# A three-stage attention kernel: six waits of the routed branch taken apart, and a causal mask moved from TensorE to VectorE

## The chip, the core and the metric

The kernel runs on one core of a Trainium2 chip. The metric is the device time of one execution in microseconds (us). A core has a matrix engine (TensorE, PE in the profile; PEld is its weight load), a vector engine (VectorE, DVE), an activation engine (ScalarE, ACT), a general engine (GpSimd, POOL) and a queue engine that starts transfers (SyncE, SP). Each runs its own list of instructions in order and waits for the others at semaphores. Matrix products land in PSUM, which has eight banks of 512 float32 numbers in each of 128 partitions.

## The reference

The input is one sequence of 2048 rows of 128 numbers. Three pieces matter here; the rest is an attention with relu weights (16 heads of 8) and a gated layer between the pieces.

```python
# routed branch: 255 of 2048 rows are chosen by a router weight, and get a layer of their own
weights = (x @ router_w)[..., 0] + router_b[0]
topv, topi = jax.lax.top_k(weights, k)
sel_idx = jnp.sort(topi[:, :kc], axis=1)
m_sel = m[bidx[:, :, None], sel_idx[:, :, None], sel_idx[:, None, :]]
sc = jnp.einsum('bhqd,bhkd->bhqk', q, kk) / np.sqrt(hd).astype(np.float32)
sc = sc + m_sel[:, None]
a = jax.nn.softmax(sc, axis=-1)
x2 = x1 + jax.nn.gelu(rmsnorm(x1, ln2) @ w1) @ w2

# second attention: 16 heads of 64, causal
q = jnp.einsum('bsm,hmd->bshd', x, W_Q) + b_Q
scores = jnp.einsum('bqhd,bkhd->bhqk', q, k) / jnp.sqrt(jnp.float32(D_HEAD))
causal = jnp.tril(jnp.ones((seq, seq), dtype=bool))
```

The masked scores go through a softmax, are multiplied with the values, and W_O maps them back to 128 numbers.

## The kernel before

The program is five blocks, one after the other; a block starts when every engine has ended the one before. `prepare` (0 to about 44.8 us) normalises, projects, and counts for each row how many router weights are larger. It also stores q and k, each as a high and a low part, to DRAM, and SyncE waits for these four stores before the block ends. `routed0` (to about 120.8 us) is the routed branch. Then come the relu attention (`attention0`), `between`, and from about 550 us `attention1`, the second attention.

**prepare.** `HIGHS_AFTER` and `LOWS_AFTER` say after which of the 16 comparisons of the counting ScalarE copies the high parts and VectorE subtracts the low parts; units 4 to 7 are those of k. Each store starts when its four parts are there.

**routed0.** VectorE makes 16 one-hot tiles (L877), and TensorE gathers the chosen rows with them (L1052). Meanwhile GpSimd sums twelve of the tiles (`tails`, L865 to 868). TensorE selects columns of the mask (L1063), ScalarE copies them out (L1010, two copies of two banks each, then kT, L1013), and TensorE selects rows (L1129) into one bank for both halves s of the queries. VectorE copies the result (L941) and adds it to the scores (L955); ScalarE takes the exponentials (L1026). Behind the last head VectorE writes the reciprocal of the sums, spread over the 8 columns of each head (L965), TensorE transposes it (L1172), ScalarE copies it out (`share`, L1033), VectorE scales (L969) and TensorE mixes (L1179). Between L1172 and the mixing TensorE also does `place(0)` to `place(3)`: transposes of the one-hot tiles (L1077) for the scatter at the end. Then come a norm with a square root on ScalarE (L1038), a product (L1193), a gelu over 1024 columns (L1040) and a product (L1199).

**attention1.** The 8 pairs of heads go through 10 groups of 4 steps each; a step is one tile of 128 keys against up to 512 queries, of both heads. TensorE's work with PSUM is a list of units (`UNIT`) that share three pairs of banks in turn: unit n may start when unit n-3 is freed. The units are scores (freed by ScalarE's exponential, L1895), projections, values, mixes, turns, and maximum tiles. A maximum tile is a tile of 128 queries against up to 512 keys (L1731); VectorE takes its row maxima (L1952) and frees the unit. These are for the pair of heads that comes next. A pair has 40 of them; 16 lie on the diagonal, four each with 128, 256, 384 and 512 columns. In a diagonal tile TensorE adds the mask to the last 128 columns with four bfloat16 products of 128 columns (L1736). VectorE also takes the reciprocal of the sums (L1973) and multiplies with it (L1976), in the same list.

A maximum tile is written (i, c) below: i the tile of queries (0 to 15), c the block of 512 keys; it is diagonal where c is i // 4.

Of the kernel before, what the change touches and what calls it, by code (L numbers as in the profile page):

```python
# [78 lines left out]
def prepare(nc, a, sh):  # L79

    with ExitStack() as ctx:
# [63 lines left out]
        HIGHS_AFTER = {2: range(NC, 2 * NC)}  # L145
        LOWS_AFTER = {1: range(0, 2), 2: range(2, NC), 10: range(NC, 2 * NC)}
# [285 lines left out]
def attention0(nc, a, sh):  # L432

    with ExitStack() as ctx:
# [78 lines left out]
        def _(pool):  # L513
# [19 lines left out]
            second_constants(nc, link, sh, sh.xnT)  # L533
# [174 lines left out]
def routed0(nc, a, sh):  # L708


    with ExitStack() as ctx:
# [106 lines left out]
        PLACE_BANK = [0, 1, 2, 3, 2, 3, 5, 6]  # L818
# [27 lines left out]
        def _(pool):  # L846
# [17 lines left out]
            pool.wait_ge(ranked, T - MT)  # L864
# [6 lines left out]
        def _(dve):  # L871
# [68 lines left out]
            dve.wait_ge(mask_taken, 1)  # L940
            link(nc.vector.tensor_copy(mask_sel[:, :, 0:SEL],  # L941
                                       bank[7].rearrange("p (s k) -> p s k", s=NS)[:, :, 0:SEL]))
# [7 lines left out]

            for n in range(H):
                if n % GH == 0:
                    dve.wait_ge(scored, n // GH + 1)
                for s in range(NS):
                    last = nc.vector.tensor_tensor_reduce(  # L955
                        out=prob[:, head(n), s, :], in0=bank[n % GH][:, s * SLOTS:(s + 1) * SLOTS],
                        in1=mask_sel[:, s, :], scale=-1.0, scalar=3.0e38, op0=ALU.add, op1=ALU.min,
                        accum_out=top[:, head(n), s:s + 1])
                last.then_inc(masked, 1)
# [15 lines left out]
            take_turned(1, bank[7])  # L975
# [5 lines left out]
            link(nc.vector.tensor_tensor(proc[:, :, :], bank[4][:, 0:NS * D].rearrange("p (s d) -> p s d", s=NS),  # L981
# [15 lines left out]
        def _(act):  # L997
# [10 lines left out]
            for n in range(2):  # L1008
                act.wait_ge(cols_taken, n + 1)
                nc.scalar.copy(mask_cols[:, 2 * n:2 * n + 2, :], sh.psum[:, 2 * n:2 * n + 2, 0:SLOTS])\  # L1010
                    .then_inc(cols_out, 1)
# [35 lines left out]
        def _(pe):  # L1047
# [92 lines left out]
            def turn_probs(n):  # L1140
# [3 lines left out]
                if n == 2:  # L1144
                    pe.wait_ge(qm_done, RES)
# [1017 lines left out]
```

## Time and profile before

| | us |
|---|---|
| median of 3 timed runs | 1413.13 (1411.38 to 1413.79) |
| the profiled execution, its own time | 1410.19 |
| its span in the trace | 1408.2 |
| PE busy | 1313.0 (93%) |
| DVE busy | 1015.9 (72%) |
| granted TensorE clock, mean | 0.982 |

The profile is of one execution. The 2 us between its own time and its span lie around the program. Busy shares are averages over stages with different limits, so the rows further down are read stage by stage: a row of the timeline gives the start, the duration, the engine, the line, what is written from what, and in brackets how long the engine had been idle before it and what ended that. The chain of waits is followed back from the last instruction, at each step to what released it.

### The profile page before, as it was taken

How to read it: one execution, taken by the hardware profiler on the slowest of the kernel's cores; microseconds unless marked ns; L12 is line 12 of the kernel's file. 1: busy time of each engine (PE TensorE's matmuls, PEld its weight loads, DVE VectorE, ACT ScalarE, POOL GpSimd, SP SyncE). 2: the span in 40 equal slices, each digit the busy share in tenths (PEclk: the TensorE clock that was granted, in tenths of full speed). 3: DMA queues.
4: the chain of work that ended last, by engine and by line, in shares of the span. 5: the costliest groups of instructions: out<-in, count | busy, mean ns of one | idle time of the engine just before them, and what ended most of it. 6: DMA issues, size and time to landing. Idle time of an engine off the chain costs nothing.

```text
span 1408.2 us, 25489 instructions
## 1 busy us (share of the span) xinstructions
PE 1313.0 (93%) x9902; PEld 674.9 (48%) x9902; DVE 1015.9 (72%) x1495; ACT 749.8 (53%) x1200; POOL 691.9 (49%) x527
## 2 busy tenths in 40 slices
PE   5778999999999987989999999999999999999897
PEld 3654222222222245555555655555555555555554
DVE  7666888888888875776766766766766666766768
ACT  5275777877777774334444444444344344344343
POOL 4301060100100010558678678677677677777671
PEclk9799999999999999999999999999999999999999
DMA  2511320000000000000000000000000000000000
GB/s 98 160 74 51 111 47 1 1 1 1 2 1 2 2 1 1 1 1 1 1 1 1 1 1 1 1 1 0 1 1 1 1 1 1 1 1 1 1 16 16
DMA packets 18166, 21.50 MB, mean 15 GB/s; under 512 B 7785, under 2 KB 15873, under 8 KB 16513
## 3 DMA queue, kind: packets, MB, share of 16 engines
q1 hardware_dynamic: 18048, 19.88, 4.6%
q8 instruction: 81, 1.33, 0.4%
q14 instruction: 37, 0.30, 0.1%
HBM read 14.63 MB, written 5.24 MB: 14 GB/s over the span
## 4 chain that ended last, share of the span: by engine, by line
PE 43%; DVE 11%; ACT 3%; issue 1%; POOL 1%; DVEq 0%; POOLq 0%; ACTq 0%
PE psum L1810 13%; PE psum L1788 12%; DVE part_max L1952 4%; PE psum L1731 4%; DVE inv L1973 4%; PE psum L1791 3%; ACT prob L1895 3%; PE psum L1769 2%; PE psum L1718 2%; PE psum L1757 2%; PE psum L1709 1%; DVE z L1976 1%; PE psum L1711 1%; PE psum L1710 1%; PE psum L1736 1%
## 5 line engine op out<-in xcount | busy, mean ns | idle before, releaser
L1698 POOL TENSOR_TENSOR acc<-acc,prob 128x1024 f32<-128x1024 f32 (+3 forms) x250 | 492.8, 1971 | 87.4 <-ACT prob L1895 57.6
L1895 ACT ACTIVATE prob<-psum 128x1024 f32<-128x1024 f32 (+1 forms) x320 | 283.3, 897 | 353.8 <-PE psum L1791 346.4
L1952 DVE TENSOR_REDUCE part_max<-psum 128x2 f32<-128x1024 f32 (+2 forms) x320 | 336.7, 1063 | 170.0 <-PE psum L1731 85.6
L696 DVE TENSOR_SCALAR w<-psum 128x512 f32<-128x512 f32 x472 | 304.7, 686 | 59.0 <-PE psum L553 46.6
L647 ACT ACTIVATE w<-psum 128x512 f32<-128x512 f32 x552 | 294.2, 600 | 85.4 <-PE psum L553 84.8
L573 PE MATMUL psum<-w,v_cols 128*32 128x512 f32 x2048 | 274.1, 608 | 0.0
L1810 PE MATMUL psum<-prob,v_pair 128*64 128x512 f32 (+3 forms) x1280 | 250.2, 532 | 0.7 <-POOL prob L1666 0.7
L1788 PE MATMUL psum<-q_hi,k_hi 64*128 64x512 f32 (+3 forms) x640 | 139.0, 430 | 30.4 <-DVE part_max L1952 21.5
L1810 PEld LDWEIGHTS psum<-prob,v_pair 128*64 128x64 f32 x1280 | 87.4, 137 | 145.2 <-issue 134.2
L1731 PE MATMUL psum<-k_hi,q_hi 64*128 64x512 f32 (+3 forms) x640 | 132.5, 411 | 6.0 <-DVE part_max L1952 4.4
L1788 PE MATMUL psum<-q_lo,k_hi 64*128 64x512 f32 (+3 forms) x640 | 119.1, 368 | 0.0
L1788 PE MATMUL psum<-q_hi,k_lo 64*128 64x512 f32 (+3 forms) x640 | 119.1, 368 | 0.0
L1791 PE MATMUL psum<-max_rows,ones_r 64*128 64x512 f32 (+3 forms) x640 | 118.7, 366 | 0.0
L1973 DVE RECIPROCAL inv<-psum 128x512 f32<-128x512 f32 x31 | 103.9, 3352 | 16.5 <-PE psum L1757 16.5
L553 PEld LDWEIGHTS psum<-q_rows,k_rows 32*128 32x128 f32 x768 | 40.3, 181 | 154.0 <-ACT w L647 148.1
L397 POOL TENSOR_SCALAR xa<-xa,rstd_j,shift_j 128x128 f32<-128x128 f32 x16 | 6.9, 449 | 209.0 <-DVE shift_j L389 209.0
L1666 POOL TENSOR_SCALAR_AFFINE_SELECT prob<-prob 128x256 f32<-128x256 f32 x128 | 53.3, 423 | 110.9 <-ACT prob L1895 110.1
L553 PE MATMUL psum<-q_rows,k_rows 32*128 32x512 f32 x768 | 101.6, 493 | 0.1
L1788 PEld LDWEIGHTS psum<-q_hi,k_hi 64*128 64x128 f32 x640 | 61.4, 188 | 78.0 <-DVE part_max L1952 47.4
L1731 PEld LDWEIGHTS psum<-k_hi,q_hi 64*128 64x128 f32 x640 | 61.2, 187 | 77.6 <-issue 40.8
L1694 POOL TENSOR_TENSOR acc<-prob 128x1024 f32<-128x1024 f32 x23 | 54.9, 2385 | 43.2 <-ACT prob L1895 41.4
L573 PEld LDWEIGHTS psum<-w,v_cols 128*32 128x32 f32 x2048 | 40.6, 108 | 63.8 <-ACT w L647 53.5
(301 smaller groups left out, 1411.3 us busy)
## 6 DMA issues: line engine op xcount, KB each, us to landing
q_rows<-q_dram SPq DMA_DIRECT2D x12, 256.0 KB
k_rows<-k_dram SPq DMA_DIRECT2D x3, 1024.0 KB
q_dram<-parts SPq DMA_DIRECT2D x2, 1024.0 KB, 4.2
k_dram<-parts SPq DMA_DIRECT2D x2, 1024.0 KB, 6.6
x<-in_L_attn_x SPq DMA_DIRECT2D x4, 256.0 KB, 4.0
mask<-in_L_ffn_attention_mask SPq DMA_DIRECT2D x1, 1024.0 KB, 6.0
x_high<-q_dram SPq DMA_DIRECT2D x4, 256.0 KB
x_low<-k_dram SPq DMA_DIRECT2D x1, 1024.0 KB
```

The costliest lines, as they stand in the source:

```text
L553: last = nc.tensor.matmul(pair_bank[n % RING][i], k_rows[group][rows, kt * P:(kt + 1) * P], q_rows[group][rows, qc * C:(qc + 1) * C], star ...
L573: last = nc.tensor.matmul(out_bank[turn % 2][h * VW:(h + 1) * VW, :], v_cols[group][:, kt, h, :], w[:, s % WR, h, :], start=(kt == 0), sto ...
L647: nc.scalar.activation(w[:, s % WR, 2 * m + i, :], pair_bank[n % RING][i], ACT.Relu)\
L696: nc.vector.tensor_scalar(w[:, s % WR, 2 * m + 1, :], pair_bank[n % RING][1], 0.0, None, ALU.max)\
L1698: nc.gpsimd.tensor_tensor(sums, sums, prob[:, s % PR, :, q0:C], ALU.add).then_inc(summed, 1)
L1731: last = nc.tensor.matmul(to[:, m, 0:n], q_hi[HALF[m], i * P:(i + 1) * P], k_hi[hp % 2][HALF[m], c * C:c * C + n], start=True, stop=not di ...
L1788: nc.tensor.matmul(to[:, m, q0:C], left[HALF[m], keys], right[HALF[m], at], start=n == 0, stop=False)
L1791: last = nc.tensor.matmul(to[:, m, q0:C], ones_r[HALF[m], :], max_rows[HALF[m], at], start=False, stop=True)
L1810: last = nc.tensor.matmul(out_bank[HALF[m], q0:C], v_pair[hp % 2][:, kt, HALF[m]], prob[:, s % PR, m, q0:C], start=kt == 0, stop=kt == (qc ...
L1895: nc.scalar.activation(prob[:, s % PR, :, q0:C], unit_both[n % RING][:, :, q0:C], ACT.Exp, scale=SCALE)\
L1952: nc.vector.tensor_reduce(part_max[:, :, i, c], unit_both[n % RING][:, :, 0:cols], AX_X, ALU.max)\
L1973: nc.vector.reciprocal(inv[:, :], side_bank).then_inc(inv_done, 1)
```

## The change

In `prepare` the k parts are made one comparison earlier on ScalarE, and three earlier on VectorE. In `routed0`: GpSimd starts its sums when all 16 one-hot tiles are there, no longer twelve; kT is copied first and the mask columns in four copies of one bank each; the mask rows of s = 0 and s = 1 go to two banks, the first scores lie between them on TensorE, and VectorE masks all four heads of s = 0 before s = 1; the reciprocal is taken of the 32 sums and a copy spreads it; two of the four first `place` units go ahead of that transpose and the other two behind the mixing; a square root on a spare cell loads ScalarE's table behind the last exponential; the gelu is taken in two halves with the products around it. Several banks are renamed to fit. In `attention1` the four bfloat16 products of a diagonal tile go, and VectorE adds a float32 mask of 128 columns, for both heads in one instruction, to the tile in PSUM. It waits for the end of this add (`link`) and then takes the maxima. The mask is built by two GpSimd instructions in place of ten.

```diff
-        HIGHS_AFTER = {2: range(NC, 2 * NC)}
-        LOWS_AFTER = {1: range(0, 2), 2: range(2, NC), 10: range(NC, 2 * NC)}
+        HIGHS_AFTER = {1: range(NC, 2 * NC)}
+        LOWS_AFTER = {1: range(0, 2), 2: range(2, NC), 7: range(NC, 2 * NC)}
...
-            pool.wait_ge(ranked, T - MT)
+            pool.wait_ge(ranked, T)
...
             dve.wait_ge(exped, H)
-            nc.vector.reciprocal(hn[:, :, :].rearrange("p s (h j) -> p s h j", j=HD0),
-                                 total[:, :, :].unsqueeze(3).to_broadcast([P, NS, H, HD0])).then_inc(share_ready, 1)
+            link(nc.vector.reciprocal(total[:, :, :], total[:, :, :]))
+            nc.vector.tensor_copy(hn[:, :, :].rearrange("p s (h j) -> p s h j", j=HD0),
+                                  total[:, :, :].unsqueeze(3).to_broadcast([P, NS, H, HD0])).then_inc(share_ready, 1)
...
+            nc.scalar.activation(idle[:, :], sh.ones[:, 0:1], ACT.Sqrt)
             act.wait_ge(share_spread, 1)
...
-            act.wait_ge(hidden, 1)
-            nc.scalar.activation(gate[:, :], sh.psum[:, 0:2, :].rearrange("p b c -> p (b c)"), ACT.Gelu_apprx_tanh)\
-                .then_inc(gated, 1)
+            for n in range(2):
+                act.wait_ge(hidden, n + 1)
+                nc.scalar.activation(gate[:, n * C:(n + 1) * C], bank[2 + n], ACT.Gelu_apprx_tanh).then_inc(gated, 1)
...
             pe.wait_ge(kT_done, 1)
-            for s in range(NS):
-                for c in range(MT):
-                    last = nc.tensor.matmul(bank[7][:, s * SLOTS:(s + 1) * SLOTS], mask_cols[:, c, s * P:(s + 1) * P],
-                                            rows(c), start=(c == 0), stop=(c == MT - 1))
-            last.then_inc(mask_taken, 1)
+            pe.wait_ge(cols_out, MT)
+            mask_slots(0)
             score(0)
+            pe.wait_ge(qm_done, RES)
+            mask_slots(1)
...
-                                            k_hi[hp % 2][HALF[m], c * C:c * C + n], start=True, stop=not diagonal)
-                if diagonal:
-                    for half in range(2):
-                        for m in range(2):
-                            last = nc.tensor.matmul(to[:, m, n - P:n], ident_b[HALF[m], half, :],
-                                                    causal[HALF[m], half, :], start=False, stop=half == 1)
+                                            k_hi[hp % 2][HALF[m], c * C:c * C + n], start=True, stop=True)
                 last.then_inc(unit_filled, 1)
...
                 dve.wait_ge(unit_filled, n + 1)
+                if c == i // TC:
+                    own = unit_both[n % RING][:, :, cols - P:cols]
+                    link(nc.vector.tensor_tensor(own, own, causal[:, :].unsqueeze(1).to_broadcast([P, 2, P]), ALU.add))
                 nc.vector.tensor_reduce(part_max[:, :, i, c], unit_both[n % RING][:, :, 0:cols], AX_X, ALU.max)\
                     .then_inc(unit_freed[n % RING], 1)
```

Three places show how the lists move. First VectorE in `attention1`, right behind a reciprocal: the last five maximum tiles of one pair of heads, (14, 3) to (15, 3), and the first two of the next. Before:

```order
L1976 TENSOR_TENSOR z<-z,inv 128x512
L1952 TENSOR_REDUCE part_max<-psum 128x2 x5
L1960 TENSOR_REDUCE neg_max<-part_max 128x2x4
L1941 SCALAR_TENSOR_TENSOR k_lo<-psum,bias,k_hi 128x512
L1944 SCALAR_TENSOR_TENSOR q_lo<-psum,bias,q_hi 128x512
L1952 TENSOR_REDUCE part_max<-psum 128x2 x2
```

The same place in the changed kernel, where the reductions are L1953 and the adds L1952:

```order
L1977 TENSOR_TENSOR z<-z,inv 128x512
L1952 TENSOR_TENSOR psum<-psum,causal 128x2x128
L1953 TENSOR_REDUCE part_max<-psum 128x2 x4
L1952 TENSOR_TENSOR psum<-psum,causal 128x2x128
L1953 TENSOR_REDUCE part_max<-psum 128x2
L1961 TENSOR_REDUCE neg_max<-part_max 128x2x4
L1939 SCALAR_TENSOR_TENSOR k_lo<-psum,bias,k_hi 128x512
L1942 SCALAR_TENSOR_TENSOR q_lo<-psum,bias,q_hi 128x512
L1952 TENSOR_TENSOR psum<-psum,causal 128x2x128
L1953 TENSOR_REDUCE part_max<-psum 128x2
L1952 TENSOR_TENSOR psum<-psum,causal 128x2x128
L1953 TENSOR_REDUCE part_max<-psum 128x2
```

Each diagonal tile has become two instructions, the second of which waits for the first. Next TensorE at the end of the routed branch's attention, from the last transposes of probabilities to the norm. Before:

```order
L1148 MATMUL psum<-ident,prob 128x128 x8
L1172 MATMUL psum<-ident,hn 128x128 x2
L1157 MATMUL psum<-mask,equal 32x256 x8
L1077 MATMUL psum<-ident,onehot 128x128 x16
L1179 MATMUL psum<-w_heads,oT 128x128 x2
L1077 MATMUL psum<-ident,onehot 128x128 x12
L1084 MATMUL psum<-ident,hn 128x128 x2
```

The same place in the changed kernel:

```order
L1160 MATMUL psum<-ident,prob 128x128 x8
L1087 MATMUL psum<-ident,onehot 128x128 x8
L1186 MATMUL psum<-ident,hn 128x128 x2
L1169 MATMUL psum<-mask,equal 32x256 x8
L1191 MATMUL psum<-w_heads,oT 128x128 x2
L1087 MATMUL psum<-ident,onehot 128x128 x20
L1094 MATMUL psum<-ident,hn 128x128 x2
```

Eight transposes of one-hot tiles (L1087) moved ahead of the transposed reciprocals, and none is left between those and the mixing (L1191). Last ScalarE, where the columns of the mask (w_heads) and kT are copied out. Before:

```order
L1004 COPY equal<-psum 128x2x4x8 x4
L1010 COPY w_heads<-psum 128x512 x2
L1013 COPY kT<-psum 128x256
L1026 ACTIVATE prob,total<-prob,top 128x256 x10
```

In the changed kernel:

```order
L1014 COPY equal<-psum 128x2x4x8 x4
L1019 COPY kT<-psum 128x256
L1022 COPY w_heads<-psum 128x256 x4
L1035 ACTIVATE prob,total<-prob,top 128x256 x10
```

The copy of kT stands ahead of the four mask copies, each of which waits for one bank only.

## Rows read from the trace of the kernel before

**Rows 1.** The page, section 4: the chain that ended last, by engine.

```profile
PE 43%; DVE 11%; ACT 3%; issue 1%; POOL 1%; DVEq 0%; POOLq 0%; ACTq 0%
```

**Rows 2.** Busy time by stretch: length, PE, PEld, DVE, ACT, POOL, clock, DMA.

```profile
760.00:860.00 100.00, 96.11 (x693) 56.89 (x689) 65.79 (x64) 42.23 (x54) 74.95 (x52) 0.98 0.00 1
```

**Rows 3.** Groups of instructions by line: the mask products.

```profile
L1736 PE MATMUL psum<-causal,ident_b 64*128 64x128 bf16 x512 | 36.9, 222 | 0.0
```

**Rows 4.** Chain of waits, 700 to 830 us: start, duration, what.

```profile
710.94 0.69 PE psum L1788 x6
...
739.64 0.13 PE psum L1736 x4
739.77 0.75 PE psum L1788 x6
```

**Rows 5.** Timeline of the routed branch, VectorE: an add of 256 elements and its follower.

```profile
100.79 0.42 DVE L971 TENSOR_TENSOR x_sel<-psum,xs 128x256 f32<-128x256 f32 x1 [1.82 <-PE psum L1179]
...
101.25 0.29 DVE L889 CUSTOM_DVE_ANT_0 hn<-x_sel 128x128 f32<-128x128 f32 x1
```

**Rows 6.** Timeline of VectorE in one lap: tiles (14, 3), (2, 0), (3, 0), (11, 2).

```profile
826.45 2.08 DVE L1952 TENSOR_REDUCE part_max<-psum 128x2 f32<-128x768 f32 x2
...
844.83 0.96 DVE L1952 TENSOR_REDUCE part_max<-psum 128x2 f32<-128x768 f32 x1 [2.12 <-PE psum L1736]
846.18 1.23 DVE L1952 TENSOR_REDUCE part_max<-psum 128x2 f32<-128x1024 f32 x1 [0.39 <-PE psum L1736]
...
897.27 1.21 DVE L1952 TENSOR_REDUCE part_max<-psum 128x2 f32<-128x1024 f32 x1
```

**Rows 7.** Timeline of TensorE: the units that wait for those tiles.

```profile
827.45 0.50 PE L1788 MATMUL psum<-q_hi,k_hi 64*128 64x512 f32 x2 [0.92 <-DVE part_max L1952]
...
845.95 0.48 PE L1788 MATMUL psum<-q_hi,k_hi 64*128 64x512 f32 x2
...
847.46 0.50 PE L1788 MATMUL psum<-q_hi,k_hi 64*128 64x512 f32 x2
...
898.54 0.50 PE L1788 MATMUL psum<-q_hi,k_hi 64*128 64x512 f32 x2 [1.86 <-DVE part_max L1952]
```

**Rows 8.** Timeline of VectorE, start of the second attention.

```profile
564.69 5.08 DVE L1952 TENSOR_REDUCE part_max<-psum 128x2 f32<-128x512 f32 x5 [1.15 <-PE psum L1736]
```

**Rows 9.** The first block's end: SyncE's waits (sum, times, longest), TensorE's last product.

```profile
SPq L81 <- DMA k_dram<-parts: 6.2, 1, 6.2
...
42.53 0.17 PE L355 MATMUL psum<-minus_b,equal 128*128 128x1 bf16 x1
```

**Rows 10.** Timelines: one-hot tiles and GpSimd's sums, and two multiplies of the second attention.

```profile
45.27 11.69 DVE L877 TENSOR_SCALAR onehot<-iota,rank 128x256 f32<-128x256 f32 x16
...
50.65 3.48 POOL L865 TENSOR_TENSOR prob<-onehot 128x1536 f32<-128x1536 f32 x1 [1.54 <-DVE onehot L877]
...
56.22 1.53 PE L1052 MATMUL psum<-xa,onehot 128*128 128x137 f32 x8 [1.15 <-DVE onehot L877]
...
857.31 0.69 DVE L1976 TENSOR_TENSOR z<-z,inv 128x512 f32<-128x512 f32 x1
...
896.18 1.17 DVE L1976 TENSOR_TENSOR z<-z,inv 128x512 f32<-128x512 f32 x1
```

**Rows 11.** Timeline of the routed branch: the mask rows.

```profile
68.77 1.53 PE L1129 MATMUL psum<-onehot,w_heads 128*128 128x256 f32 x6 [1.04 <-ACT kT L1013]
```

**Rows 12.** Timeline of the routed branch: from the last head to the norm.

```profile
95.16 1.75 DVE L965 RECIPROCAL hn<-total 128x256 f32<-128x256 f32 x1 [1.04 <-ACT prob L1026]
...
98.34 1.97 PE L1077 MATMUL psum<-ident,onehot 128*128 128x128 f32 x16
...
100.14 0.61 PE L1179 MATMUL psum<-w_heads,oT 128*128 128x128 f32 x4
```

**Rows 13.** The same timeline: the gelu, and the first product of the next block.

```profile
107.17 1.02 ACT L1040 ACTIVATE w_heads<-psum 128x1024 f32<-128x1024 f32 x1 [3.27 <-PE psum L1193]
...
120.86 0.73 PE L553 MATMUL psum<-x_high,x_low 32*128 32x512 f32 x6 [2.12 <-PEq L711]
```

More of the change, by code:

```diff
@@ L949, in take_probs, with mask_scores @@
                     .then_inc(probT_by_dve, 1)
-            for n in range(H):
-                if n % GH == 0:
-                    dve.wait_ge(scored, n // GH + 1)
-                for s in range(NS):
[L955 to L959, printed above, removed]
+            def mask_scores(n, s):
+                return nc.vector.tensor_tensor_reduce(
+                    out=prob[:, head(n), s, :], in0=bank[n % GH][:, s * SLOTS:(s + 1) * SLOTS],
+                    in1=mask_sel[:, s, :], scale=-1.0, scalar=3.0e38, op0=ALU.add, op1=ALU.min,
+                    accum_out=top[:, head(n), s:s + 1])
+            for s in range(NS):
+                dve.wait_ge(mask_taken, s + 1)
+                link(nc.vector.tensor_copy(mask_sel[:, s, 0:SEL], MASK_BANK[s][:, 0:SEL]))
+                dve.wait_ge(scored, 1)
+                for n in range(GH):
+                    last = mask_scores(n, s)
+                    if s == NS - 1:
+                        last.then_inc(masked, 1)
+            for n in range(H):
+                if n >= GH:
+                    if n % GH == 0:
+                        dve.wait_ge(scored, n // GH + 1)
+                    mask_scores(n, 0)
+                    mask_scores(n, 1).then_inc(masked, 1)
                 if n % GH == GH - 1:
@@ L974, in _ @@
             rms_scale(1, x1)
-            take_turned(1, bank[7])
+            take_turned(1, bank[5])
             for u in range(NC, 2 * NC):
@@ L1007, in _ @@
             last.then_inc(v_taken, 1)
[L1008 to L1011, printed above, removed]
             act.wait_ge(qk_turned, 1)
             nc.scalar.copy(kT[:, :], bank[7][:, 0:SLOTS]).then_inc(kT_done, 1)
+            for c in range(MT):
+                act.wait_ge(cols_taken, c + 1)
+                nc.scalar.copy(mask_cols[:, c, :], bank[c][:, 0:SLOTS]).then_inc(cols_out, 1)
             def take_probs(n):
@@ L1123, in score, with mask_slots @@
                 last.then_inc(scored, 1)
-            pe.wait_ge(cols_out, 2)
-            pe.wait_ge(kT_done, 1)
-            for s in range(NS):
-                for c in range(MT):
-                    last = nc.tensor.matmul(bank[7][:, s * SLOTS:(s + 1) * SLOTS], mask_cols[:, c, s * P:(s + 1) * P],
-                                            rows(c), start=(c == 0), stop=(c == MT - 1))
-            last.then_inc(mask_taken, 1)
+            def mask_slots(s):
+                for c in range(MT):
+                    last = nc.tensor.matmul([bank[7], bank[6]][s][:, 0:SLOTS], mask_cols[:, c, s * P:(s + 1) * P],
+                                            rows(c), start=(c == 0), stop=(c == MT - 1))
+                last.then_inc(mask_taken, 1)
+            pe.wait_ge(kT_done, 1)
+            pe.wait_ge(cols_out, MT)
+            mask_slots(0)
             score(0)
+            pe.wait_ge(qm_done, RES)
+            mask_slots(1)
             def wait_probs(n):
@@ L1168, in _ @@
                         weigh(n // GH - 1)
+            for u in range(2):
+                place(u)
             pe.wait_ge(share_ready, 1)
@@ L1174, in _ @@
             weigh(RES - 1)
-            for u in range(NC):
-                place(u)
             pe.wait_ge(oT_done, 1)
@@ L1192, in _ @@
             for f in range(FT):
[L1193 removed]
+                last = nc.tensor.matmul(bank[2 + f // 2][:, (f % 2) * SLOTS:(f % 2 + 1) * SLOTS], w1[:, f * P:(f + 1) * P],
                                         hnT[:, :], start=True, stop=True)
[L1195 to L1199 removed]
+                if f % 2:
+                    last.then_inc(hidden, 1)
+            for f in range(FT):
+                pe.wait_ge(gated, f // 2 + 1)
+                for s in range(NS):
+                    last = nc.tensor.matmul(bank[4 + s][:, 0:D],
                                             gate[:, f * SLOTS + s * P:f * SLOTS + (s + 1) * P], w2[:, f, :],
```

52 lines of the change are left out of this document (16 added, 36 removed).

## The prediction

> **What bounds the kernel now.** I read the chain of waits first, then the busy time by stretch, then the timelines of the second attention and of the routed branch. The reader is to see that TensorE is nearly the bound of the second attention, but not alone: a stretch of 100 us there has 96 us of TensorE at clock 0.98, and 66 us of VectorE [rows 2], yet VectorE holds 11% of the whole chain [rows 1], some 155 of 1408 us. The average hides that VectorE is late at certain tiles. So the question is, tile by tile, whether TensorE has something to do until the reduction is done. In the routed branch every engine waits for another, and the next block starts right behind its end [rows 13]: what its chain loses, the program loses.
>
> **The mask products, TensorE's side.** There are 512 of them for 128 diagonal tiles [rows 3]. Their busy time of 36.9 us overlaps their neighbours. On the chain the four of a tile have 0.13 us, and the first six score products behind them take 0.75 where six behind an ordinary tile take 0.69 [rows 4]. So a tile gives back 0.13 + 0.06 = 0.19 us, and all of them at most 128 x 0.19 = 24 us, where TensorE doesn't then wait.
>
> **The add, VectorE's side.** An add of 256 elements from PSUM and SBUF takes 0.42 us, and its linked follower starts at 101.25, 0.04 behind its end [rows 5]. That one writes SBUF; the new one writes back into PSUM, which no row of an engine shows. Bounds: 0.42 + 0.04 = 0.46 per tile if the write costs the same; above, the 0.69 of a multiply of 512 elements with 0.04, 0.73, as if each element were handled twice; below, an add hidden wholly behind a reduction is excluded, since the maxima wait for it and it waits for TensorE. I take 0.46, the row of the same size. For 128 tiles that is 59 us, of which the part counts that TensorE waits for.
>
> **One lap.** A lap is one pair of heads, about 104 us, with 16 diagonal tiles. From start and end of each reduction and the start of the unit three later I read the room behind a tile.
> - Behind a reciprocal VectorE is already late. (14, 3) ends at 826.45 + 0.95 = 827.40 and TensorE, idle for 0.92, starts at 827.45. (11, 2) ends at 898.48, and TensorE, idle for 1.86, starts at 898.54 [rows 6, 7]. Each costs the whole 0.46: 0.92.
> - (2, 0) and (3, 0): the first ends at 844.83 + 0.96 = 845.79, 0.16 ahead of the unit at 845.95; the second at 847.41, 0.05 ahead of 847.46 [rows 6, 7]. The first fill comes 0.13 earlier and its reduction 0.46 later, the next reduction queues behind it, and the ordinary tile after them hands on 0.37. TensorE's own savings are already in that.
> - (5, 1), (6, 1) and (10, 2) repeat the pattern, with 0.07, 0.14 and 0.06 of room. In the first two much is won back by the saved products of (6, 1) and (7, 1), net 0.13; behind (10, 2) TensorE soon waits for an exponential anyway, net 0.21.
> - The other nine have 0.3 us of room or more. Four give back 0.19, 0.19, 0.19 and 0.11. At the rest TensorE already waits for the reduction before, or for ScalarE, and its saved 0.19 turns into idle time; they give 0.05 together.
>
> Sum: 0.92 + 0.37 + 0.13 + 0.21 - 0.68 - 0.05 = +0.90 us per lap. Seven laps of this kind: +6.3.
>
> **The first maxima**, those of pair 0, are dense, and VectorE runs them back to back: five take 5.08 us without a pause [rows 8]. Here adds go straight into the chain. The four ahead of the first scores cost 4 x 0.46 = 1.84; (5, 1) and (6, 1), in that row, 0.92; (10, 2) and (11, 2) 0.83, with the turn that waits for them; (14, 3) 0.46; savings 0.2. Sum +3.9. The second attention gets 6.3 + 3.9 = +10.2 us. GpSimd's shorter making of constants lies far from any wait: nothing.
>
> **The routed branch and what is ahead of it.**
> - *k parts earlier.* SyncE waits 6.2 us for the second k store; TensorE's last product ends at 42.70 [rows 9], and the next block's one-hot tiles start at 45.27 [rows 10], 0.4 behind its first instruction. The store is issued some 3 us earlier, so TensorE becomes the later one: -1.9 (with a barrier of 0.25). Bounds: 0, if the two stores, now closer, only share the transfer engines; -2.1. I take -1.9, since the first store starts 2 us earlier too.
> - *GpSimd waits for 16 tiles.* The sum at 50.65 takes 3.48 us, and the 16 one-hot tiles take 11.69 though most take 0.34; TensorE is idle 1.15 us for the last [rows 10]. Without the stall the gather ends 1.74 us earlier, the upper bound. But this sum and the three shorter ones behind it now run beside the norm of the chosen rows. A multiply of two SBUF tiles takes 0.69, and another of the same size 1.17 beside GpSimd's additions [rows 10], so that norm can stall as the tiles did: its two squares and its scaling each meet a sum, and some 1.5 us go back. I take -0.25.
> - *Mask columns and rows.* TensorE is idle for 1.04 us until kT is copied behind both mask copies, at 68.77 [rows 11]. With kT first and the last bank's copy half as wide (some 0.4 us instead of two copies of together 0.95) about half of that idle time is left; the two halves make up the same work, and the exponentials behind it fill ScalarE. -0.55.
> - *Reciprocal, two places ahead, table.* The reciprocal (1.75) shrinks to some 0.8 with its copy, but eight transposes now stand ahead, 0.98 (half of the 1.97), so this wins only 0.2. What wins is that the mixing, at 100.14, no longer stands behind 16 transposes [rows 12]: it starts when `oT` is ready, near 98.9. The table load ahead of the square root makes the root follow at once. -1.27 together. The places moved behind the mixing are done before the norm, as before. If the table load, which stands ahead of ScalarE's copy of `share`, were later than the product it lies beside, 0.3 would go back.
> - *Gelu in halves.* Of 1.02 us [rows 13] and the second half of the products, 1.05 lies beside each other now. -1.05. The bound on the other side is 0, if the first half doesn't start before TensorE ends both.
>
> Sum: -1.9 - 0.25 - 0.55 - 1.27 - 1.05 = -5.0 us; by the bounds, -2 to -7.
>
> At the GpSimd wait a rule speaks against the change. The Trainium skill says (SBUF — State Buffer, Who interferes with whom) that VectorE, in a two-port mode or with two SBUF inputs against a GpSimd instruction that reads SBUF, and GpSimd hold one pair of ports in turn, each for a whole instruction. By that rule the two squares and the small scaling are blocked for one sum each and the gain is about 0.2; without it, 1.74. The 3.48 us stall agrees with it for the one-hot tiles. The same rule leaves the new add alone, since it has one input in SBUF.
>
> **Total.** +10.2 - 5.0 = +5.2 us on the profiled execution: 1410.2 + 5.2 = 1415.4. That execution was 2.9 us under the median of the runs (1413.1), so for a median I predict 1418.
>
> **The rivals.**
> 1. *VectorE's waits eat the saving, as above.* +5, 1418.
> 2. *TensorE's saving wins.* If the three units in flight cover the add wherever the room is over 0.05, TensorE keeps its 0.19 at 110 tiles (-21) and pays 0.46 only behind reciprocals and in the first maxima (7 x 0.92 + 3.9 = +10.3): about -10, with the branch -15, 1398. Halfway, with half of the tight tiles covered, about -5 in all, 1408. For it: 96% busy [rows 2]. Against: TensorE is idle just ahead of units that wait for reductions [rows 7], and a unit can't start on a tile that isn't freed.
> 3. *A wash.* The add's cost as taken, but savings kept at a few more tiles (each 0.19 of which eight in a lap are kept is 1.5 us, 7 laps -5): 1413.
> 4. *The write into PSUM is dear.* At 0.73 per tile, the eight tight tiles of a lap pay 0.27 more: 7 x 8 x 0.27 = +15, and +3 in the first maxima: 1436. Between, at 0.55, 1424.
> 5. *The routed branch gives nothing*, because the moved copies and sums meet others: +10, 1423.
>
> **How the numbers follow.** Chances: rival 1 0.42, rival 2 with its halfway 0.17, rival 3 0.24, rival 4 0.09, rival 5 0.08. No change is within 0.2%, 2.8 us, about what a measurement of this kernel can tell. Faster is rival 2, 0.17; same is rival 3, 0.24; slower is the rest, 0.59. The likeliest case has its own range of 1414 to 1423. The range goes to half of rival 2, 1408.5, and to the middle of rival 4, 1425, and leaves out 2 in 10.
>
> **What would show it.** In the profile of the changed kernel: adds of 0.42 us on VectorE with the reduction 0.04 behind; TensorE's idle time ahead of score units put down to part_max about doubled; a lap about 1 us longer than before, the first maxima 4 us longer; the branch ended near 115.5 instead of 120.6, the block before it near 43; TensorE's mixing near 1.2 us closer to the last head; squares of the first norm stretched by GpSimd's sums. Wrong would be: laps shorter than before (then TensorE's side was undersized or kept), an add over 0.5 us, or a branch that ends within 2 us of before.

## The result, and the profile after

The changed kernel takes 1422.37 us (median of five runs, 1420.76 to 1428.17), the kernel before 1411.38 in runs beside it (1410.73 to 1413.79). The ratio is 1.008, with a 95% interval of 1.0059 to 1.0101: slower by 8 to 14 us. The forecast was 1418 in a range of 1408.5 to 1425.

The profiled execution has a span of 1421.5 us, 13.3 more than before. Second attention, from its first projection to TensorE's last product: 857.2 us before, 878.0 now (+20.8). It starts at 540.35 instead of 547.91 (-7.6). So both parts have the sign that was forecast (+10.2 and -5.0), and both are larger.

The chain of waits by engine, of the changed kernel, to be read against [rows 1]:

```profile
PE 38%; DVE 19%; ACT 3%; issue 1%; POOL 1%; DVEq 0%; ACTq 0%; POOLq 0%
```

Five points of TensorE's share have gone, and VectorE has won eight. Its groups of instructions, by line: engine, operation, tiles, count, then busy time, mean ns and idle time ahead with what ended it.

```profile
L1953 DVE TENSOR_REDUCE part_max<-psum 128x2 f32<-128x1024 f32 (+2 forms) x320 | 336.7, 1064 | 73.0 <-PE psum L1734 67.1
L1786 PE MATMUL psum<-q_hi,k_hi 64*128 64x512 f32 (+3 forms) x640 | 136.6, 423 | 53.4 <-DVE part_max L1953 41.2 <-ACT prob L1893 5.8 <-DVE max_rows L1968 2.8
L1952 DVE TENSOR_TENSOR psum<-psum,causal 128x256 f32<-128x256 f32 x128 | 54.9, 429 | 68.8 <-PE psum L1734 67.3
```

The second row is the first score product of each unit. TensorE was idle ahead of it for 53.4 us, 41.2 of them put down to a reduction. The same row of before:

```profile
L1788 PE MATMUL psum<-q_hi,k_hi 64*128 64x512 f32 (+3 forms) x640 | 139.0, 430 | 30.4 <-DVE part_max L1952 21.5 <-ACT prob L1895 3.9 <-DVE max_rows L1967 2.8
```

Behind a reciprocal the add stands whole in the way. Timelines of VectorE and TensorE of the changed kernel at tiles (14, 3) and (11, 2), the places of [rows 6, 7]:

```profile
830.25 0.42 DVE L1952 TENSOR_TENSOR psum<-psum,causal 128x256 f32<-128x256 f32 x1
830.71 2.09 DVE L1953 TENSOR_REDUCE part_max<-psum 128x2 f32<-128x768 f32 x2
...
902.46 0.42 DVE L1952 TENSOR_TENSOR psum<-psum,causal 128x256 f32<-128x256 f32 x1
902.92 1.23 DVE L1953 TENSOR_REDUCE part_max<-psum 128x2 f32<-128x1024 f32 x1
```

```profile
831.73 0.50 PE L1786 MATMUL psum<-q_hi,k_hi 64*128 64x512 f32 x2 [1.56 <-DVE part_max L1953]
...
904.20 0.50 PE L1786 MATMUL psum<-q_hi,k_hi 64*128 64x512 f32 x2 [2.54 <-DVE part_max L1953]
```

TensorE's idle times there were 0.92 and 1.86 us; they are 1.56 and 2.54, so 0.64 and 0.68 more. That is more than the 0.46 of an add: the rest is time that TensorE saved ahead of the wait and now waits away. The reduction starts 0.04 behind the end of the add.

Two laps of the changed kernel and two of before, by stretch, columns as in [rows 2]. A lap runs here from the first score product of a pair of heads to that of the next.

```profile
784.71:891.59 106.88, 99.81 (x670) 58.60 (x670) 76.44 (x85) 45.08 (x57) 79.64 (x54) 0.98 0.00 1
891.59:997.26 105.67, 98.49 (x672) 57.49 (x671) 76.43 (x85) 45.10 (x57) 79.61 (x54) 1.00 0.00 1
```

```profile
781.91:886.85 104.94, 101.02 (x740) 60.22 (x736) 69.79 (x69) 45.19 (x57) 79.65 (x54) 0.98 0.00 1
886.85:990.65 103.80, 99.91 (x740) 58.92 (x736) 69.81 (x69) 45.19 (x57) 79.61 (x54) 1.00 0.00 1
```

Length is the first number, the granted clock the third from the end. In each kernel the lap with a mean clock of 0.98 holds one stretch at half clock (1.2 GHz in place of 2.4) and is 1.1 to 1.2 us longer than the lap at 1.00. Compared at clock 1.00, the change costs 105.67 - 103.80 = 1.87 us per lap, and TensorE's busy time falls by 1.42. Of the laps of pairs 1 to 6 three held a half clock before, and five do now.

The opening, from the first projection to the first score product, is the other surprise: it takes 14.84 us, and took 11.09. The changed kernel's TensorE in the opening, and the clock there:

```profile
547.58 1.52 PE L1722 MATMUL psum<-w_heads,xnT 128*128 128x128 f32 x8 [0.57 <-DVE part_max L1953]
550.90 0.45 PE L1741 MATMUL psum<-ident,neg_max 128*128 128x128 f32 x1 [1.80 <-DVE neg_max L1961]
551.15 3.64 PE L1839 MATMUL psum<-wo,prob 128*128 128x128 f32 x16
```

```profile
541.00:548.00 7.00, 4.45 (x22) 2.77 (x21) 4.96 (x10) 3.08 (x5) 0.00 (x0) 1.00 0.02 4
548.00:555.00 7.00, 5.20 (x26) 4.71 (x26) 3.39 (x6) 0.58 (x1) 0.00 (x0) 0.52 0.00 0
```

TensorE waits for VectorE, longer than before, and then runs the 16 bias products at half clock: 3.64 us. Before they took 2.01:

```profile
556.72 2.01 PE L1841 MATMUL psum<-wo,prob 128*128 128x128 f32 x16
```

Last, the routed branch. The changed kernel's GpSimd and VectorE where the chosen rows are normed:

```profile
52.31 1.81 POOL L866 TENSOR_TENSOR prob<-prob 128x768 f32<-128x768 f32 x1
54.19 0.87 POOL L867 TENSOR_TENSOR prob<-prob 128x256 f32<-128x256 f32 x1
```

```profile
52.51 0.44 DVE L884 COPY xs<-psum 128x274 f32<-128x274 f32 x1 [3.70 <-PE psum L1062]
52.99 1.27 DVE L889 CUSTOM_DVE_ANT_0 hn<-xs 128x128 f32<-128x128 f32 x1
...
54.52 0.57 DVE L893 TENSOR_SCALAR square<-square 128x2 f32<-128x2 f32 x1
```

The first square takes 1.27 us (its twin behind it 0.28) and ends 0.14 us behind GpSimd's sum; the scaling takes 0.57 (0.17 before) and ends 0.03 behind the next sum. The one-hot tiles, 11.69 us before [rows 10], take 6.35. The stage from the first one-hot tile to the copy of the gathered rows, of before and then of the changed kernel:

```profile
45.30:57.80 12.50, 10.58 (x67) 10.18 (x67) 11.78 (x19) 0.80 (x1) 10.28 (x13) 0.79 0.70 214
```

```profile
42.40:52.50 10.10, 9.41 (x67) 9.41 (x67) 6.41 (x18) 0.78 (x1) 7.13 (x11) 0.80 0.65 208
```

The branch's successor starts at 113.56, where the forecast had about 115.5 and before had 120.86 [rows 13].

### The profile page after: what moved, and what is told of

The parts are those of the page before. It is cut to its first block, busy times and chain, and to the rows that moved or that the text cites. A ratio compares the mean times of both kernels' runs of the same rounds, so it can differ in the third digit from the quotient of the medians.

```text
span 1421.5 us, 24589 instructions
## 1 busy us (share of the span) xinstructions
PE 1304.1 (92%) x9390; PEld 665.2 (47%) x9390; DVE 1064.6 (75%) x1625; ACT 749.3 (53%) x1204; POOL 688.2 (48%) x519
## 4 chain that ended last, share of the span: by engine, by line
PE 38%; DVE 19%; ACT 3%; issue 1%; POOL 1%; DVEq 0%; ACTq 0%; POOLq 0%
PE psum L1808 12%; PE psum L1786 11%; DVE part_max L1953 8%; DVE inv L1974 5%; PE psum L1734 3%; PE psum L1789 3%; ACT prob L1893 2%; PE psum L1767 2%; PE psum L1722 2%; DVE psum L1952 2%; PE psum L1713 1%; DVE z L1977 1%; PE psum L1755 1%; PE psum L1715 1%; PE psum L1714 1%
## 5 line engine op out<-in xcount | busy, mean ns | idle before, releaser
L1953 DVE TENSOR_REDUCE part_max<-psum 128x2 f32<-128x1024 f32 (+2 forms) x320 | 336.7, 1064 | 73.0 <-PE psum L1734 67.1
L696 DVE TENSOR_SCALAR w<-psum 128x512 f32<-128x512 f32 x472 | 305.2, 687 | 58.2 <-PE psum L553 44.6
L1786 PE MATMUL psum<-q_hi,k_hi 64*128 64x512 f32 (+3 forms) x640 | 136.6, 423 | 53.4 <-DVE part_max L1953 41.2
L1952 DVE TENSOR_TENSOR psum<-psum,causal 128x256 f32<-128x256 f32 x128 | 54.9, 429 | 68.8 <-PE psum L1734 67.3
```

Source lines behind the costliest of these rows:

```text
L696: nc.vector.tensor_scalar(w[:, s % WR, 2 * m + 1, :], pair_bank[n % RING][1], 0.0, None, ALU.max)\
L1786: nc.tensor.matmul(to[:, m, q0:C], left[HALF[m], keys], right[HALF[m], at], start=n == 0, stop=False)
L1953: nc.vector.tensor_reduce(part_max[:, :, i, c], unit_both[n % RING][:, :, 0:cols], AX_X, ALU.max)\
```

## Experiments

All of them are compared with the kernel before on the same chip. "Laps" are those of pairs 1 to 6, at clock 1.00 unless said.

**1. The change in two halves.** `routed_only` is the kernel before with the edits of the prepare block and the routed branch, `add_only` the kernel before with those of the second attention.

> Only the edits of the prepare block and the routed branch; the second attention keeps TensorE's mask products. Theory (the branch's gain is kept, and the loss is all in the second attention): 1411.4 - 7.5 = 1404, the second attention starts near 540.4 and lasts as before (547.9 to its end). Rival (the two parts are not independent, the earlier branch only moves a wait): within 2 us of 1411.

> Only the second attention's change. Theory (the loss is all there, 20.9 us in the profile of the changed kernel): 1411.4 + 20.9 = 1432, a steady lap 1.85 us longer. Rival (half of the 20.9 is an accident of when the earlier branch lets the second attention start): 1411.4 + 10 = 1421, as the prediction had it.

`routed_only`: 1405.37 against 1411.04 us, ratio 0.9959 (0.9946 to 0.9973): -5.7. `add_only`: 1432.0, ratio 1.0146 (1.0126 to 1.0165): +21. The loss is all in the second attention, and it hardly hangs on when that starts: it lasts 876.4 us in the profile of `add_only` and 878.0 in the changed kernel's. Their sum is +15.3, and the change as a whole gives +11.0. The difference is that of three or four half clocks at 1.2 us; that these are the cause was not shown.

**2. Products and adds, each with and without.** Without either (`neither`, whose maxima of diagonal tiles then leave the mask out) and with both (`both`), on the earlier branch:

```diff
--- changed kernel, for neither
-                if c == i // TC:
-                    own = unit_both[n % RING][:, :, cols - P:cols]
-                    link(nc.vector.tensor_tensor(own, own, causal[:, :].unsqueeze(1).to_broadcast([P, 2, P]), ALU.add))
```

> The changed kernel without the add: the maxima of diagonal tiles are taken without the causal mask, so that part of the computation is left out. Theory (a reduction that starts at once behind its fill gives TensorE no new wait, but the saved products count only where TensorE itself was late, at the four or five tiles of a lap): routed_only - 5 to -9, near 1397, and the laps of this kernel against the changed one show the whole price of the adds, 25 us. Rival (all 128 tiles keep their 0.19): routed_only - 24 = 1380.

> The earlier branch, TensorE's mask products and VectorE's add at every diagonal tile. Theory (most of the saved product time was turned into waiting, so to have the products back costs little, about 0.1 at a tile in those places where VectorE's handover is late, 4 to 8 us): changed kernel + 6 = 1428. Rival (the saved products count in full): + 24 = 1446.

`neither`: 1398.39 us, ratio 0.9916 (0.9902 to 0.9929). `both`: 1429.74, 1.0130 (1.0114 to 1.0147). One lap of each, `neither` first, then `both`, then `routed_only`:

```profile
778.02:880.78 102.76, 98.07 (x670) 57.19 (x670) 69.81 (x69) 45.20 (x57) 79.67 (x54) 1.00 0.00 1
```

```profile
787.62:894.10 106.48, 100.58 (x739) 58.91 (x736) 76.37 (x85) 45.12 (x57) 79.81 (x54) 1.00 0.00 1
```

```profile
988.05:1091.84 103.79, 99.84 (x738) 58.95 (x736) 69.79 (x69) 45.25 (x57) 79.70 (x54) 1.00 0.00 1
```

| a lap at clock 1.00 | no add | add |
|---|---|---|
| no products | 102.76 | 105.67 |
| products | 103.79 | 106.48 |

The 16 adds cost 2.9 us per lap without the products and 2.7 with them. The products cost 1.0 and 0.8, that is 0.06 and 0.05 us per tile in the mean, waits included; the prediction had 0.19 where TensorE doesn't wait. The two prices hardly meet: trading one for the other is -1.0 + 2.9 = +1.9.

**3. Tile by tile.** The step at a tile is how much later TensorE starts the next diagonal tile, of two kernels, less how much later it started this one. Median of pairs 2 to 6; (7, 1), one of the prediction's "other nine", stands where its saving was used up:

| tiles | prediction | changed less `routed_only` | `neither` less `routed_only` |
|---|---|---|---|
| (14, 3) | +0.46 | +0.48 | 0.0 |
| (11, 2) | +0.46 | +0.46 | half clocks hide it |
| (2, 0) + (3, 0) | +0.37 | +0.34 | -0.30 |
| (5, 1) + (6, 1) + (7, 1) | +0.13 | +0.37 | -0.23 |
| (10, 2) | +0.21 | +0.33 | -0.13 |
| the other eight | -0.73 | -0.21 | -0.45 |

Two kernels ask whether the first two rows and the last hold when only such tiles get the add. They are `routed_only` with the rows of `BY_ADD` on VectorE and the rest on TensorE; `causal_f` is a float mask like the changed kernel's. A third such kernel has the rows whose steps fell:

```diff
+        BY_ADD = (1, 4, 8, 9, 12, 13)      # roomy;  late: (11, 14);  hybrid: (0, 7, 15)
-                diagonal = c == i // TC
+                diagonal = c == i // TC and i not in BY_ADD
+                if c == i // TC and i in BY_ADD:
+                    own = unit_both[n % RING][:, :, cols - P:cols]
+                    link(nc.vector.tensor_tensor(own, own, causal_f[:, :].unsqueeze(1).to_broadcast([P, 2, P]), ALU.add))
```

> routed_only, with VectorE's add only at tiles of rows 1, 4, 8, 9, 12 and 13, which have 0.3 us of room or more behind their reduction. Prediction's step: a roomy tile gives back up to 0.19. Theory now (TensorE's next unit there waits for a reduction or an exponential that the mask products don't delay, so a saved product becomes idle time): a lap without half clock lasts 103.8 + 0.0 to 0.1, no gain. Prediction's: 0.2 to 0.4 shorter, 103.5.

> routed_only, with VectorE's add only at tiles of rows 11 and 14, whose reductions stand behind a reciprocal. Theory and prediction's step agree: 0.46 each, a lap without half clock of 103.8 + 0.95 = 104.75. Rival (part of the price comes from the tiles around them, which now keep their products): 0.2 to 0.6.

> routed_only, with VectorE's add only for tiles of rows 0, 7 and 15, whose steps got 0.13, 0.21 and 0.11 us shorter in each lap of the changed kernel; the other 13 keep TensorE's products. Theory (the price is set tile by tile by the room behind the reduction): 0.45 per lap, 7 laps, -3: 1402. Rival (the shorter steps only gave back what the tile before had lost, and alone they gain nothing or cost): 1405 to 1410.

`roomy`: lap 103.94 (six tiles without products, and nothing gained; the step +0.07 is all at (9, 2)), 1406.67 us, ratio 0.9973 (0.9962 to 0.9984). Its trace shows where the saved products went: behind (1, 0) TensorE waits 0.30 us for an exponential in place of 0.17, behind (13, 3) 0.28 for a reduction in place of 0.15, and `neither`, without any add, has the same two waits. `late`: lap 104.82, +1.03 for two adds, a little over twice 0.46, and each further lap has a half clock too, 105.8. Its 1416.32 us, ratio 1.0044 (1.0028 to 1.006), is, by the ratios (0.0085 apart), 12 us above `routed_only`, and the changed kernel is 17 above it (0.0121). The spans of the profiled executions give 7.1 and 16.3, and the laps 1.03 of 1.88. So 16 of the 128 adds do about half of the harm (0.4 to 0.7 of it, by which of these one takes). One lap with and one without a half clock:

```profile
674.88:779.70 104.82, 99.60 (x730) 58.73 (x728) 70.69 (x71) 45.23 (x57) 79.59 (x54) 1.00 0.01 1
779.70:885.52 105.82, 100.66 (x730) 59.88 (x728) 70.69 (x71) 45.22 (x57) 79.57 (x54) 0.98 0.00 1
```

`hybrid`: 1401.63, ratio 0.9943 (0.9931 to 0.9955), lap 103.5, against the 103.35 expected. Rows 0 and 15 keep their 0.13 and 0.10 there, row 7 only 0.12 of its 0.21: part of that had been won back from row 6. In pair 0 the same adds cost 1.1 (0.85 of it in the opening).

**4. The half clock of the opening.**

```diff
-                for m in range(2):
-                    last = nc.tensor.matmul(to[:, m, 0:n], q_hi[HALF[m], i * P:(i + 1) * P],
+                for _ in range(3 if hp == 0 and i in (2, 3) else 1):
+                    for m in range(2):
+                        last = nc.tensor.matmul(to[:, m, 0:n], q_hi[HALF[m], i * P:(i + 1) * P],
...
-                for j in range(TC):
+                for j in list(range(TC)) * (2 if (hp, c) == (0, 0) else 1):
```

> The changed kernel, with TensorE kept at work in the opening of the second attention while it would wait for VectorE: the products of tiles (2, 0) and (3, 0) of pair 0 are issued three times and those of the first value unit twice, into the same places. Theory (the wait for the adds lets the granted clock fall to 0.50 there, and the half clock costs 1.7 of the opening's 3.75 us): no half clock between 547 and 555, the 16 bias products take 2.0 us instead of 3.64, the opening lasts 14.84 - 1.7 = 13.1, the kernel 1420.7. Rival (the half clock comes from something else, or the opening waits for another): opening 14.8 or longer, 1422.4.

The opening lasts 12.98 us instead of 14.84. TensorE there, and the clock, of `clock_fill`:

```profile
550.23 1.77 PE L1735 MATMUL psum<-k_hi,q_hi 64*128 64x384 f32 x12 [0.94 <-DVE q_lo L1943]
552.09 2.05 PE L1722 MATMUL psum<-w_heads,xnT 128*128 128x128 f32 x16
555.41 0.30 PE L1742 MATMUL psum<-ident,neg_max 128*128 128x128 f32 x1 [1.27 <-DVE neg_max L1962]
555.55 2.01 PE L1840 MATMUL psum<-wo,prob 128*128 128x128 f32 x16
```

```profile
550.00:557.00 7.00, 5.39 (x42) 4.43 (x43) 5.69 (x11) 0.59 (x1) 0.00 (x0) 1.00 0.00 0
```

With work that nobody needs in place of the wait, the clock stays at 1.00 and the bias products are back at 2.01 us. The opening is left 1.89 longer than before: the four adds, 4 x 0.46 = 1.84. The whole kernel took 1420.92 us, ratio 1.0075 (1.0061 to 1.009). That is the expected number, but 1.5 us can't be told from nothing between two kernels here, and the profile has another side: behind the opening, from 562.6, 10.2 us ran at half clock, where the changed kernel had 3.4 from 565.3. From the first score product to that of the next pair it took 123.0 us, against 122.6. The fill kept the clock up in the opening alone, and the rest of pair 0 won nothing.

The longer wait for the adds isn't what it takes for the half clock, either. `neither` has no add and the same wait of 1.23 us ahead of these products as the kernel before, and they run at half clock there too; its opening lasts 13.11 us, against 11.11 in `routed_only`:

```profile
550.10 0.45 PE L1741 MATMUL psum<-ident,neg_max 128*128 128x128 f32 x1 [1.23 <-DVE neg_max L1958]
550.34 3.66 PE L1839 MATMUL psum<-wo,prob 128*128 128x128 f32 x16
```

`both`, with the adds and the mask products, has the half clock as well (14.84 us). So the half clock came where TensorE waited longer for adds and kept its mask products, and also where it lost them and had no add to wait for. It did not come where TensorE had extra work. What decides it stays open.

**5. The reciprocal's place.** In front of (11, 2) VectorE holds a 3.36 us reciprocal. In `total_first` (on `routed_only`) and `total_first_add` (on the changed kernel) TensorE makes the product that it waits for before a value unit and not behind it:

```diff
+                early = k % LAPS == 0 and k - 1 in ENDS
+                if early:
+                    total(ENDS.index(k - 1))
                 for unit in whole_phase(k):
                     fill(unit)
-                if k - 1 in ENDS:
+                if k - 1 in ENDS and not early:
```

> routed_only, with the product of the sums (whose reciprocal VectorE runs ahead of tile (11, 2)) issued one value unit earlier in each lap, by 1.1 us. Theory (the longest idle time of a lap, 1.87 us, is VectorE's 3.36 us reciprocal ahead of a reduction, and the half clock in most laps follows it): a lap gets 1.1 shorter, those with a half clock there 1.2 more: 6 x 1.1 + 4 x 1.2 = 11, 1394. Rival (the idle time moves to the next wait, as the saved products' did): under 2 us gained.

> The changed kernel with the product of the sums one value unit earlier, as in total_first. Theory: the add behind the reciprocal still costs its whole 0.46, since VectorE is still late there, so a lap is 103.0 + 1.86 = 104.8; the wait ahead of tile (11, 2)'s follower shrinks from 2.5 to 1.5 us and the half clock behind it goes: 1422.4 - 0.9 x 7 - 1.2 x 5 = 1410. Rival (with the reciprocal out of the way the adds are covered): laps of 104.0, 1404.

`total_first`: 1394.47 us, ratio 0.9885 (0.9871 to 0.99). TensorE's wait at (11, 2), and a lap:

```profile
891.44 0.50 PE L1800 MATMUL psum<-q_hi,k_hi 64*128 64x512 f32 x2 [0.86 <-DVE part_max L1967]
```

```profile
880.64:983.56 102.92, 100.04 (x738) 58.75 (x736) 70.05 (x69) 45.22 (x57) 79.84 (x54) 1.00 0.00 1
```

The wait is 0.86 in place of 1.86, and each of the laps of pairs 1 to 6 is at clock 1.00. By the ratios (0.0074 apart) one product's place in seven laps is worth 10 us. At clock 1.00 a lap is only 0.8 shorter, 103.0 against 103.8, where the expectation had 1.1; the other half of the gain is the half clock, which `routed_only` has in five of these six laps. `total_first_add`: 1415.24, ratio 1.0042 (1.0029 to 1.0055), 5 us over the expectation in time; its laps are as expected, 104.72 to 104.79 but for one with a half clock. Against `total_first` the step at (11, 2) is +0.47 and the sum per lap +1.78. So the adds are not covered once the wait is shorter; their price doesn't change. Its profiled execution is 10.0 us shorter than the changed kernel's, near the 12 expected, although its pair 7 has a longer half clock; why its median is not stays open.

**6. The prepare block and GpSimd's wait alone.**

```diff
-        HIGHS_AFTER = {2: range(NC, 2 * NC)}
-        LOWS_AFTER = {1: range(0, 2), 2: range(2, NC), 10: range(NC, 2 * NC)}
+        HIGHS_AFTER = {1: range(NC, 2 * NC)}
+        LOWS_AFTER = {1: range(0, 2), 2: range(2, NC), 7: range(NC, 2 * NC)}
...
-            pool.wait_ge(ranked, T - MT)
+            pool.wait_ge(ranked, T)
```

> The kernel before with two edits only, the k parts earlier in the prepare block and GpSimd's wait for all 16 one-hot tiles. Read from the profile by stage: first one-hot tile, copy of the gathered rows, mask rows. Theory: first tile near 43.4 (-1.9, by four profiles with the edit 42.4 to 43.5); from first tile to mask rows 23.5 before and 22.1 with all edits, of which GpSimd's wait gives about 0.8 (2.0 to 2.4 us of stall gone, 1.5 back in the stretched squares) and the mask edits 0.55. Prediction's numbers: 0.25 and 0.55.

1408.0 us, ratio 0.9984 (0.9974 to 0.9994). By stages of the profiles, in us, which is where the six edits can be told apart:

| | first one-hot tile | to first exponential | heads | to mixing | to next block |
|---|---|---|---|---|---|
| before | 45.27 | 29.26 | 20.40 | 5.21 | 20.72 |
| `add_only` (branch as before) | 45.55 | 29.26 | 21.40 | 5.20 | 20.72 |
| `kparts_pool` | 42.97 | 28.37 | 21.35 | 5.20 | 20.72 |
| changed | 42.36 | 28.05 | 19.99 | 3.81 | 19.35 |
| `routed_only` | 43.41 | 28.07 | 22.79 | 3.81 | 19.35 |

**7. What the runs point to.** `best` joins `total_first` with the adds of `hybrid` from the second pair of heads on, where they are not in the chain.

> routed_only, the product of the sums one value unit earlier, and VectorE's add at tiles of rows 0, 7 and 15 from the second pair of heads on (in the first pair the adds stand in the chain). Theory: 0.35 per lap, 7 laps, on total_first: 1394.5 - 2.5 = 1392. Rival (the earlier sums took the room away that the three adds used): 1394 to 1397.

1389.05 us against 1409.95, ratio 0.9856 (0.984 to 0.9871): 1.4% faster than before and, by the ratios, 2.2% faster than the changed kernel. Against `total_first` a lap gives the 0.35 that were expected. A lap:

```profile
877.72:980.35 102.63, 99.74 (x727) 58.46 (x724) 71.38 (x72) 45.22 (x57) 79.90 (x54) 1.00 0.00 1
```

## Why the prediction was right, and by how much it was off

The mechanism held: VectorE's adds cost more than TensorE's products gave back, and the routed branch paid for part of it. The two terms were both too small (+10.2 against +20.8, -5.0 against -7.6 in the profiles), and partly made up for each other: a forecast of +5 came out as +11. That 1418 lies within 4.4 us of the median owes something to luck, too. The profiled execution that it was built on was 2.9 us under its median, and I added that; the five runs of the comparison put the kernel before at 1411.4, only 1.2 above it, and the profiled execution of the changed kernel lay 1.2 above its own median.

- *The add, 0.46.* Right: 0.429 us in the mean, the reduction 0.04 behind. All 128 lie between 0.419 and 0.433 us, 94 of them with GpSimd at work beside them, as the prediction had it for an add with one input in SBUF. A write into PSUM costs no more than one into SBUF, so rival 4 is out.
- *Behind a reciprocal, 0.46 each.* Right, 0.48 and 0.46.
- *(2, 0) + (3, 0), +0.37.* Right, +0.34.
- *"The other nine ... Four give back 0.19, 0.19, 0.19 and 0.11".* This is the step that failed, 0.52 of the 0.88 us per lap that are missing by tiles. I took 0.19 from two pieces of one chain [rows 4] and let four tiles keep it. Without products a tile that gives back anything gives 0.11 to 0.18 (two give 0.03 and 0.05), and beside an add only (0, 0) and (15, 3) of the other eight keep 0.13. `roomy` has six tiles with room and gains nothing: TensorE's next unit waits there for a reduction or an exponential of another unit, and a shorter fill only makes that wait longer (0.17 to 0.30 us, 0.15 to 0.28). Only (9, 2) could give 0.17, and the add there takes more than that back. Room behind a reduction says at best that an add costs nothing; it doesn't say that TensorE can use what it saves.
- *(5, 1) to (7, 1), +0.13, and (10, 2), +0.21.* Too small by 0.24 and 0.12, for the same reason: the saved products "won back" less.
- *Seven laps, +6.3.* It is 7 x 1.87 = 13.1, and the laps of pairs 1 to 7 took 13.5 in the profile, with half clocks on either side.
- *The first maxima, +3.9.* They cost 7.4. The four adds ahead of the first scores were sized right (1.89 measured beside 1.84). What was missing is TensorE's clock: 1.86 of the opening's 3.75 us went when TensorE was kept busy, and without the adds `neither` still lost 2.0 there. The rest of pair 0 cost 3.6 against the 2.1 forecast; it held one stretch at half clock before and two in the changed kernel, and what they cost there wasn't measured apart.
- *k parts earlier, -1.9.* Right: -2.3 in the profile of `kparts_pool`, and a first one-hot tile between 42.0 and 44.6 in the 12 profiles with the edit, 43.1 in the mean.
- *GpSimd's wait, -0.25.* It gives -0.9. The step had two sides. The give-back was about right in the changed kernel, 0.98 at one of the two squares and 0.40 at the scaling. It hangs on timing: in `kparts_pool`, where the -0.9 was measured, the squares took 0.30 and 0.28 and only the scaling was stretched (0.57). The Trainium skill's rule (SBUF — State Buffer, Who interferes with whom) had called for the stretching, and the changed kernel's trace agrees: both stretched instructions end within 0.14 us of the end of a sum of GpSimd's. What was undersized is the gain: 2.4 us earlier in the changed kernel, 1.4 in `kparts_pool`, against an upper bound of 1.74 that I drew from the stall alone. The rest fits TensorE's clock. An estimate: by the mean clocks of the stage it ran (1 - 0.79) x 2 x 12.5 = 5.2 us of it at half clock before, 4.0 in the changed kernel and 6.0 in `kparts_pool` (mean clock 0.73), and half of each difference takes 1.74 to 2.3 and to 1.3. A bound from one stall left that out.
- *Mask columns and rows, -0.55.* -0.3 against `kparts_pool` in the profile; in others with the edit the stage took 28.7, +0.4. Not settled, and small.
- *Reciprocal and places, -1.27.* From last exponential to mixing, -1.40 in every profile.
- *Gelu halves, -1.05.* From mixing to the next block -1.37 in every profile, the earlier table load included.
- *The sum of the branch, -5.0.* `routed_only` measures -5.7, within its bounds. The -7.3 of the changed kernel's profile is the sum of a row of that table, -2.9 - 1.2 - 0.4 - 1.4 - 1.4, and `routed_only`'s own profile has +2.4 at the heads, where the edits change only banks and the order of the masks; the changed kernel has the same edits and -0.4, so the +2.4 is not theirs.

Of the signs named beforehand, the doubled idle time, the stretching (of one square and the scaling), the branch's end and TensorE's mixing were seen. The lap came out longer by 1.9 where 1 was said, the first maxima by 7.4 where 4 was said.

## What to carry to other kernels

To move work from a bound engine to one with idle time, price it at each hand-over and twice: what the receiving engine adds where the giving one waits for it, and what the giving one can do with the time it saves. Here the second was a third of what a chain of waits suggested, since most saved products stood ahead of another wait. And look at the longest wait first: one product issued 1.1 us earlier, ahead of a reciprocal, gained nearly twice what all six edits of the branch did (10 us against 5.7).

## What the runs showed of the hardware

- *A wait can cost more than itself.* In or right behind TensorE's wait at (11, 2) the granted clock fell to 0.50 in 4 of 7 laps before (1.86 us of waiting), in 4 of 7 of the changed kernel (2.54), and in none where it was 0.86. One more lap of the changed kernel has it behind the 1.56 us at (14, 3). A half clock in a lap costs 1.0 to 1.4 us. Over all 14 profiles, the laps of pairs 1 to 7:

| wait at (11, 2), us | profiles | laps with a half clock there |
|---|---|---|
| 0.84 to 0.88 | `total_first`, `best` | 0 of 14 |
| 1.49 to 1.52 | `total_first_add` | 1 of 7 |
| 1.86 to 1.89 | before, `routed_only`, `hybrid`, `roomy`, `kparts_pool` | 21 of 35 |
| 2.06 to 2.55 | changed, `add_only`, `neither`, `both`, `clock_fill`, `late` | 18 of 42 |

So a longer wait was not followed more often, and the same wait of 2.5 us was followed in 5 of 7 laps of `late` and in 1 of 7 of `clock_fill`. What tells these laps apart no run shows. The Trainium skill (TensorE: Matmul & The Clock Gate, HAM oscillation — how this bites in real kernels) tells of a clock that falls in the waits between bursts of products. The trace agrees in kind, but the waits of that section are for transfers and last some 3 to 5 us, and here 1.5 to 2.5 us for VectorE were enough. `clock_fill` kept the clock up with useless products in the opening, and not behind it.
- *It is also part of the play between runs.* The slowest of the changed kernel's five runs, 1428.17 us, had a mean granted clock of 0.975, the other four 0.978 to 0.981. The heads of the routed branch, with the same instructions, took 20.0 us in the three profiles without a half clock there, and 22.8 in `routed_only` at a mean clock of 0.86:

```profile
71.00:95.00 24.00, 18.49 (x160) 11.93 (x161) 15.74 (x66) 19.53 (x71) 0.00 (x0) 0.86 0.23 90
```

- *The busy time of small products says little of what they cost.* The mask products have 0.22 us each [rows 3], 14 us for the 64 of a lap, but they overlap. Where nothing waited behind them the four of a tile cost 0.11 to 0.18 us together (`neither` against `routed_only`), and 1.0 per lap in all, since behind most tiles TensorE had to wait anyway.
